# Two token tiles placed by matrix multiplies instead of by indirect DMA in an attention and mixture-of-experts kernel, and three copies moved from ScalarE to VectorE

## The reference

```python
# layer 0: attention, 16 heads of 8 features, no projections
xh = x.reshape(B, T, 16, 8)
c = xh - mean(xh, axis=1)
attn = softmax(c @ c.T per head) @ xh
x = layernorm(x + attn)
# layer 1: experts, E=64, K=8, NG=8, TG=4, CAP=128
scores = sigmoid(x @ gate.T)              # routing: top 4 of 8 groups, then top 8 experts
w = scores[top8] / scores[top8].sum() * 2.5
# each expert takes its first 128 tokens in token order ("pos" < CAP), the others are dropped
h  = silu(xe @ w1.T) * (xe @ w3.T)        # xe: expert x slot x feature, F = 64
ye = h @ w2.T
out = sum over experts of w * ye at the token  +  shared expert (silu, 128 wide)
x = layernorm(x + out)
```

## Time and profile before

| engine | busy us | share of span |
|---|---|---|
| PE | 415.4 | 75% |
| DVE | 378.3 | 69% |
| ACT | 365.9 | 66% |
| POOL | 351.1 | 64% |

### The profile page before, as it was taken

The page is one execution under the profiler, slowest core; times in us unless marked ns, Lnnn a source line. Parts: engine busy times, 40 slices in busy tenths (PEclk is TensorE's granted clock), DMA queues, the critical chain, the costliest instruction groups (busy, mean ns, idle before and its releaser), DMA issues.

```text
span 550.8 us, 9934 instructions
## 1 busy us (share of the span) xinstructions
PE 415.4 (75%) x3461; PEld 185.7 (34%) x3476; DVE 378.3 (69%) x1390; ACT 365.9 (66%) x486; POOL 351.1 (64%) x374
## 2 busy tenths in 40 slices
PE   3799998999898898898899889645699988740000
PEld 2323333333333333333333322123566666530000
DVE  7632769769769768768868638579877887730095
ACT  2699998998998898898998999610223322210056
POOL 3500000677777777777777777777768778888454
PEclk9699999999999999999999999965999999975555
DMA  3499990111000000000100100102366656334796
GB/s 95 139 220 222 349 388 20 52 40 46 24 6 21 14 3 19 12 3 2 27 3 2 26 3 1 24 2 63 78 121 101 112 92 96 36 36 38 150 291 194
DMA packets 71771, 43.69 MB, mean 79 GB/s; under 512 B 11859, under 2 KB 70964, under 8 KB 71329
## 3 DMA queue, kind: packets, MB, share of 16 engines
q1 hardware_dynamic: 51744, 36.18, 24.0%
q0 software_dynamic: 19968, 6.75, 10.5%
HBM read 21.27 MB, written 41.24 MB: 113 GB/s over the span
## 4 chain that ended last, share of the span: by engine, by line
DVE 29%; PE 23%; POOL 16%; ACT 14%; issue 9%; DMA 7%; ACTq 0%; DVEq 0%; POOLq 0%; SPq 0%
POOL records L571 10%; ACT large L1005 9%; PE PV L743 7%; PE S L727 5%; POOL sums L588 5%; DVE large L1587 4%; DMA sums<-centred,target 4%; PE M L645 3%; DVE LR L1261 2%; DVE centred L1644 2%; DMA records<-rec,index 2%; ACT OT L992 1%; PE M L674 1%; DVE last_stats L1672 1%; PE M L668 1%
## 5 line engine op out<-in xcount | busy, mean ns | idle before, releaser
L571 POOL DMA_INDIRECT records<-rec,index x224 | 225.4, 1006 | 141.0 <-DVE index L1404 70.4
L1005 ACT ACTIVATE large<-S,shift 128x1024 f32<-128x1024 f32 x256 | 273.4, 1123 | 23.3 <-PE S L727 21.1
L743 PE MATMUL PV<-large,V 128*9 128x512 f32 x1024 | 135.2, 600 | 0.0
L588 POOL DMA_INDIRECT sums<-centred,target x64 | 99.3, 1552 | 24.9 <-issue 12.2
L727 PE MATMUL S<-LR 64*128 64x512 bf16 x512 | 100.7, 392 | 13.4 <-ACT large L1005 9.0
L727 PEld LDWEIGHTS S<-LR 64*128 64x128 bf16 x512 | 24.6, 93 | 155.1 <-ACT large L1005 98.5
L863 PE MATMUL S<-large 128*128 128x512 bf16 (+1 forms) x189 | 42.6, 375 | 10.0 <-DVE large L1587 6.7
L1261 DVE COPY LR<-M 128x1024 bf16<-128x1024 bf16 x49 | 33.4, 681 | 16.9 <-PE M L645 16.9
L1587 DVE TENSOR_SCALAR large<-slot_c,large 128x128 bf16<-128x128 bf16 x256 | 43.7, 283 | 0.0
L1057 ACT COPY AK<-S 128x512 f32<-128x512 f32 (+1 forms) x17 | 9.5, 560 | 33.6 <-PE S L871 33.6
L863 PEld LDWEIGHTS S<-large 128*128 128x128 bf16 x204 | 19.1, 100 | 29.6 <-issue 9.8
(11 more groups left out here) (207 smaller groups left out, 672.1 us busy)
## 6 DMA issues: line engine op xcount, KB each, us to landing
records<-blank SPq DMA_DIRECT2D x1, 6176.0 KB, 32.2
large<-sums SPq DMA_DIRECT2D x24, 256.0 KB, 5.4
X<-records SPq DMA_DIRECT2D x15, 386.0 KB, 4.4
sums<-blank SPq DMA_DIRECT2D x2, 2112.0 KB
large<-L_ffn_w_dram SPq DMA_DIRECT2D x2, 2048.0 KB, 11.0
records<-rec,index POOLq DMA_INDIRECT x224, 2.1
X<-L_attn_x_dram SPq DMA_DIRECT2D x8, 256.0 KB, 2.9
w2s<-L_ffn_w_dram SPq DMA_DIRECT2D x1, 2048.0 KB, 17.5
```

What stands on the lines that cost most here:

```text
L571: pool.indirect_dma_start(records, bass.IndirectOffsetOnAxis(ap=index[:, i * TOP + k:i * TOP + k + 1], axis=0), rec[:, i, :], None, bounds ...
L588: pool.indirect_dma_start(sums[n % SUMS], bass.IndirectOffsetOnAxis(ap=target[:, u, i:i + 1], axis=0), ye[:, u, i, :], None, bounds_check= ...
L743: mm = pe.matmul(PV[g % 2][32 * i:32 * i + VCOLS, :], V[:, b % 2, 2 * c + k, QUAD * g + i, :], E[:, u % 2, i, k, :], start=c == 0 and k == ...
L1005: nc.scalar.activation(E[:, u % 2, 2 * (i // 2):2 * (i // 2) + 2, i % 2, :], S[:, 2 * (n % 2):2 * (n % 2) + 2, :], ACT.Exp, bias=shift[:, ...
```

## The change

The last two token tiles of batch 6 are no longer scattered. `scatter` issues 16 DMAs for batch 6 instead of 32, and `scatters_for` counts two tiles. Instead, `place_x` and `find_rows` go over 6 tiles (`PLACED`) instead of 4. VectorE prepares the two tiles in the last attention period (`late_tiles`, 12 instructions), and ScalarE builds their 0/1 matrix (`late_hot`): for each tile and expert the absolute difference of slot row and slot (`Abs`, with the slot as a per-partition operand), then one `Relu(1 - x)` over the whole step. The splitting of batch 7's weights in three parts is done before step 0 for 12 experts only and for the other 52 during steps 1 to 3 (`first_rows`, `far_rest`, `far_low` and two ScalarE copies). The store into `Z` now comes behind that splitting, and the matrix of step 1 is built inside step 0. The parts are kept in `Z` and `slot_of` in the memory of `AK`. In every attention period the three copies named above go from ScalarE to VectorE.

```diff
@@ constants
+LATE = 2
+PLACED = LATE + TILES
+HOTS = 4
+FIRST_WV = 3
-NORM_SLOT, X1T_SLOT, EXP_SLOT, SIGMOID_SLOT = 3, 5, 6, 7
-ACT_TAKES = {6: 15}
+NORM_SLOT, EXP_SLOT, SIGMOID_SLOT = 3, 6, 7
-VALUE_SLOT = 12
@@ scatters_for, scatter
-            sent = TILES * min(expert + 1, TOP)
+            sent = (TILES - LATE) * min(expert + 1, TOP)
...
+                tiles = TILES - LATE if p == BATCHES - 2 else TILES
                 for k in range(TOP):
-                    for i in range(TILES):
-                        n = k * TILES + i
+                    for i in range(tiles):
+                        n = k * tiles + i
@@ TensorE: place_x, find_rows
-                wait_next(pe, hot, s + 1)
-                if s == 0:
-                    pe.wait_ge(x_split, 4)
-                for k in range(PARTS):
-                    for i in range(TILES):
+                wait_next(pe, hot_late, s + 1)
+                for i in range(PLACED):
+                    if i >= LATE:
+                        wait_next(pe, hot, s * TILES + i - LATE + 1)
+                    if s == 0 and i == 0:
+                        pe.wait_ge(late, LATE_STEPS)
+                    if s == 0 and i == LATE:
+                        pe.wait_ge(x_split, 4)
+                    for k in range(PARTS):
                         pe.matmul(S[:, u % 2, 0:n * CAP], x_parts[:, k, i, :],
...
+                if s == FIRST_WV + 1:
+                    pe.wait_ge(wv_far, 6)
                 for e in range(experts_of(s)):
-                    for i in range(TILES):
+                    for i in range(PLACED):
@@ ScalarE: attention period
-                    if slot == VALUE_SLOT and b + 1 < BATCHES:
...
-                        build_v(b + 1)
-                    if phase != "last":
-                        for j, at in ACT_TAKES.items():
-                            if slot == at:
-                                take_turned(phase, b, j)
...
-                        if slot == X1T_SLOT:
-                            copy_x1T(phase, b)
@@ ScalarE: the matrix of the two tiles
+            def late_hot(s, u):
+                n = experts_of(s)
+                if s == 0:
+                    act.wait_ge(unit_weighed, UNITS * BATCHES)
+                    act.wait_ge(late, LATE_SLOTS)
+                if s >= HOTS:
+                    wait(act, found_done, s - HOTS + 1)
+                for i in range(LATE):
+                    for e in range(n):
+                        k = STEP_FIRST[s] + e
+                        ins = nc.scalar.activation(one_hot[:, u % HOTS, i, e, :], slot_c[:, :], ACT.Abs,
+                                                   bias=slot_of[:, i, k:k + 1])
+                ins.then_inc(late_far, 1)
+                wait(act, late_far, s + 1)
+                both = one_hot[:, u % HOTS, 0:LATE, 0:n, :]
+                nc.scalar.activation(both, both, ACT.Relu, bias=1.0, scale=-1.0).then_inc(hot_late, 1)
+
             copy_quad(BATCHES - 1, QUADS - 1)
             norm_start(BATCHES - 1)
+            late_hot(0, 0)
             copy_x1T("epilogue", BATCHES)
             exp_logits("epilogue", BATCHES, BATCHES - 1)
             exp_gate("epilogue", BATCHES, BATCHES - 1)
+            late_hot(1, 1)
             gate_sigmoid(BATCHES - 1)
+            late_hot(2, 2)
@@ ScalarE: expert steps
                 if s + 1 < STEPS:
                     copy_x(s + 1, s + 1)
                     exp_step(s + 1, s + 1)
+                if s + 1 == FIRST_WV - 1:
+                    act.wait_ge(wv_far, 2)
+                    nc.scalar.copy(part_of(FAR, TILES_7, 0), wv32[:, :, :, FAR]).then_inc(wv_far, 1)
+                if s + 1 == FIRST_WV:
+                    act.wait_ge(wv_far, 4)
+                    nc.scalar.copy(part_of(FAR, TILES_7, 1), wv_rest[:, :, :, FAR]).then_inc(wv_far, 1)
+                if s + 3 < STEPS:
+                    late_hot(s + 3, s + 3)
@@ VectorE: attention period
+                if with_post:
+                    copy_x1T(phase, b)
+                if with_prep:
                     take_turned(phase, b, 1)
...
+                if phase == "last":
+                    late_tiles(p, t)
                 if with_prep:
                     take_turned(phase, b, 5)
+                    build_v(b + 1)
                     prep_shift(phase, b, q, w.step, w.after)
...
                 if with_prep:
+                    take_turned(phase, b, 6)
                     take_turned(phase, b, 7)
@@ VectorE: before and in the expert steps
             one_hot_step(0, 0)
+            last_record(p, t)
             post_shared_out("epilogue", BATCHES, p)
-            last_record(p, t)
-            one_hot_step(1, 1)
...
-            take_weights(0, 0)
             for s in range(STEPS):
                 add_one(s, s)
+                if s == 0:
+                    one_hot_step(1, 1)
+                    take_weights(0, 0)
+                if s == 1:
+                    first_rows(BATCHES - 1, lambda name, ins: ins.then_inc(wv_far, 1), FAR)
+                if s == FIRST_WV - 1:
+                    far_rest()
+                if s == FIRST_WV:
+                    far_low()
                 silu_step(s, s)
+                if s < EARLY_STEPS:
+                    weigh_step(s, s)
                 if s + 2 < STEPS:
                     one_hot_step(s + 2, s + 2)
-                weigh_step(s, s)
+                if s >= EARLY_STEPS:
+                    weigh_step(s, s)
                 if s + 1 < STEPS:
                     take_weights(s + 1, s + 1)
```

More of the change, by code:

```diff
@@ L308, in post_norm_block @@
         x_split = sem("x_split")
+        late = sem("late")
+        hot_late = sem("hot_late")
+        late_far = sem("late_far")
+        wv_far = sem("wv_far")
         pos_done = sem("pos_done")
@@ L979, in build_v @@
                                tokens_of(X, b).rearrange("p (i h d) -> p i h d", i=TILES, h=HEADS)).then_inc(v_built, 1)
-            def take_turned(phase, b, j):
-                bank, n = job(phase, b, f"lr{j}")
-                wait(act, written[bank], n + 1)
-                nc.scalar.copy(LR[:, j, :, :].rearrange("p a t -> p (a t)"), Mb[bank]).then_inc(read[bank], 1)
             def copy_quad(b, g):
@@ L1279, in post_x1, with copy_x1T @@
                                                       ALU.subtract, ALU.mult))
+            def copy_x1T(phase, b):
+                bank, n = job(phase, b, "xt")
+                wait_next(dve, written[bank], n + 1)
+                v.tensor_copy(x1T[:, :], M[bank][:, :]).then_inc(read[bank], 1)
             def post_shared(phase, b, p, t):
@@ L1546, in last_slot @@
                 dve.wait_ge(pos_read, 1)
-                t.step("slot", v.scalar_tensor_tensor(slot_of[:, :, :], ie(mask), -float(CAP), ie(pos), ALU.mult, ALU.add))
+                t.step("slot", v.scalar_tensor_tensor(slot_of[:, TILES_7, :], ie(mask), -float(CAP), ie(pos),
+                                                      ALU.mult, ALU.add))
             def last_record(p, t):
@@ new lines, in first_rows @@
+            def first_rows(p, step, experts):
+                ie = lambda a: a[:, :].rearrange("p (i e) -> p i e", i=TILES)
+                n = experts.stop - experts.start
+                step("recw", v.tensor_tensor(wv32[:, 0, :, experts], ie(scores)[:, :, experts],
+                                             wsum[:, :].unsqueeze(2).to_broadcast([P, TILES, n]), ALU.mult))
+                token = record_of(p)[0][:, :, TOK_COL].unsqueeze(2).to_broadcast([P, TILES, n])
+                step("row", v.scalar_tensor_tensor(wv32[:, 1, :, experts], ie(pos)[:, :, experts], float(ALL_TOKENS),
+                                                   token, ALU.add, ALU.subtract))
@@ L1581, in one_hot_step @@
                     wait(dve, post, post_at(BATCHES - 1, "slot"))
[L1582 to L1584 removed]
+                if s >= HOTS:
+                    wait(dve, found_done, s - HOTS + 1)
+                for i in range(LATE, PLACED):
                     for e in range(n):
                         own = slot_of[:, i, STEP_FIRST[s] + e:STEP_FIRST[s] + e + 1]
[L1587 to L1588 removed]
+                        ins = v.tensor_scalar(one_hot[:, u % HOTS, i, e, :], slot_c[:, :], own, None, ALU.is_equal)
+                    ins.then_inc(hot, 1)
             split_x(p, t)
```

117 lines of the change are left out of this document (81 added, 36 removed).

## The result

The changed kernel takes 568.42 us (median of four runs, 567.44 to 569.91), the kernel before 552.71 us beside it: 1.029 times as long, 95% interval 1.025 to 1.033. The profiled execution took 568.53 us with a span of 566.7 us. The forecast was 567 us.

What follows compares the result with a forecast made beforehand. The end was taken to hang on POOL's last add, through the adds' start and POOL's 7.4 us a step. Later adds, +16.2 us, with the copies' -1.0 gave +15.2 on 552.3: 567.5, forecast 567 us, range 549 to 575.

Steps and rivals of the forecast that it cites:

- Part 1: POOL, batch 6: sixteen scatters less free POOL at 372.3 instead of 393.4 us; alone worth nothing.
- Part 2: Attention periods: three copies leaving ScalarE gain only in the first period, -1.0 us (bounds -13.3 to +3).
- Part 3: Last attention period: VectorE's twelve preparing instructions, 4.9 us, fall where it waits for PE; value 0, bounds 0 to +2.
- Part 4: Step 0: the store into Z comes 3.0 us later; first add at 396.8 us, +3.1.
- Part 5: Expert steps: ScalarE's matrix joins the dependency ring, which becomes 8.2 us (7.5 to 9.0), above POOL's 7.4.
- L: Expert steps: length of the nine new ScalarE instructions per step, 3.5 us, bounds 2.8 to 4.3.
- Steps 1 to 3: Early expert steps, each with one matrix in its path: silu of step 3 at 418.5 us.
- The sum: Whole kernel: last add starts at 532.2 instead of 516.02 us, +16.2; with Part 2 +15.2.
- A: Rival: ScalarE bounds the attention periods, so all three copies come back in seven periods; 555.2 us, chance 0.12.
- B: Rival: POOL stays the bound of the expert steps, with a matrix of 2.7 us; 549 us, chance 0.15.
- D: Rival: end unchanged, scatters were hidden beside VectorE and matrices fit ScalarE's idle time; 552 us, chance 0.06.
- C: Rival: step ring longer still, by the two-operand price or PE falling to half clock; 578 us, chance 0.07.

Runs made afterwards that it cites:

- all scatters: The changed kernel with all 32 scatters of batch 6 on POOL again, PE's placing kept: 568.94 us.
- second Relu: The changed kernel with a second Relu over the same 1024 columns in each of ScalarE's matrices: 586.76 us.
- matrix behind the copy: The changed kernel with ScalarE building step s+3's matrix behind the copy of X, ahead of the up product's exponential: 558.98 us.
- copies alone: The kernel before with only the three copies of a period moved from ScalarE to VectorE: 553.93 us, ratio 1.001.
- early-split version: Matrix behind the copy, plus step 0 placed early, matrices of steps 1, 3 and 4 moved or cut, far weights split before step 0: 549.10 us.

## Why the prediction was right, step by step

**Part 1, sixteen scatters less.** Right: the last one starts at 371.35 us, and POOL then waits 24 us. Worth nothing in the changed kernel (all scatters: 568.94), worth 5.0 us where nothing else is late (554.14 against 549.10), through the loads and not through POOL.

**Part 2, the copies.** The period stays at 42.5 us, as argued from the releasers. My -1.0 us for the first period isn't confirmed: 553.93 us, interval 0.998 to 1.004. A few of the runs scatter by 3 us, so a gain of half a microsecond remains possible.

**Part 3, the two tiles.** Right. VectorE works on them from 347.78 to 352.3 us, 4.5 us, and the last quad is read after only 0.60 us of idle time for PE:

```profile
353.47 0.26 DVE L1175 RECIPROCAL rden<-PV 128x16 f32<-128x16 f32 x1 [0.60 <-PE PV L770]
```

**Part 4, step 0.** The first add comes at 396.35 us; predicted was 396.8 less part 2, 395.8. The first scatter of this execution came 1.4 us earlier than in the earlier trace rows, so I count from there: PE's start was predicted at 286.7 us and is at 286.4, the first add was predicted at 299.7 and is at 300.7. The start is right, but the placing took 1.0 us longer:

```profile
382.03 6.43 PE L884 MATMUL S<-large,Z 128*128 128x512 bf16 x18 [5.01 <-DVE Z L1415]
```

I had given the half clock 7 matmuls, as the earlier trace rows have it, and 5.4 us in all. But PE now waits 5.01 us before it starts, instead of 2.38, and 11 matmuls run at a pitch of 0.43 us. The up product ends at 295.4 us all the same, as predicted: PE's start is 0.4 us early, and I had put 0.7 us too much behind the placing. The 1.0 us of the first add arises behind the up product: I had left out its exponential (`add_one` starts 0.5 us after the product's end), and the first add starts 1.13 us after the weighing does (395.22 us) where it is 0.61 us in a full step; why it is longer there the trace doesn't say.

**Part 5, the ring.** Right in place and size: predicted 8.2 us (7.5 to 9.0), measured 8.00 in ten of the eleven rings and 8.89 in the first; L predicted 3.5, measured 3.43; an `Abs` predicted 0.39, measured 0.389; PE's own step predicted 7.25, measured 7.24 where nothing holds it. The second Relu shows that ScalarE's time goes into the ring one to one (9.09 us where the clock stays full), the matrix behind the copy that it is the place and not the amount.

By the Trainium skill, page "ScalarE: Activation LUTs", section "What ACT_TABLE_LOAD costs", an ACTIVATE with one pointer operand takes about 280 + 0.833 N ns, which by estimate is 387 ns for 128 columns; the trace agrees with its 389 ns.

**Steps 1 to 3** came out 2.8 us late. The silu of step 3 was predicted at 418.5 us and runs from 418.99 to 419.87 us. It is the end that has to be compared, since the 3.1 us counted from the last silu to the weighing hold only the compares and that weighing; from the first scatter it is 324.2 us instead of 321.4. Inside there are two terms that I had mis-sized or left out. Timeline of ScalarE and PE:

```profile
396.11 0.28 ACT L1093 ACTIVATE X<-S 128x128 f32<-128x128 f32 x1 [1.47 <-PE S L920]
...
401.05 0.80 PE L933 MATMUL M<-w2s,AK 64*128 64x128 f32 x4 [2.68 <-DVE AK L1727]
...
403.55 1.12 PE L920 MATMUL S<-AK,large 128*64 128x128 f32 x8 [0.25 <-ACT AK L1085]
...
404.88 1.57 ACT L1112 CAST Z<-Z 128x416 bf16<-128x416 f32 x1
406.08 2.49 ACT L1062 ACTIVATE large<-slot_c,AK 128x128 bf16<-128x128 bf16 x8
```

Each copy of the far weights takes 1.57 us where I had put 0.5, and delays the `Abs` behind it by 1.20 us: 1.4 us more in all. And behind PE's wait of 2.68 us its clock is at half: down product, turning, finding and up product of 128-column pieces take 0.80, 1.22, 0.51 and 1.12 us, where the run with the matrix behind the copy has 0.49, 0.71, 0.45 and 0.66 us: 1.3 us that no term of mine held. The up product of step 1, ahead of both, ended at 300.4 us from the first scatter, as predicted.

The same happens once more in the first of the eleven full rings, from the silu of step 3 to that of step 4:

```profile
419.93 0.71 PE L933 MATMUL M<-w2s,AK 64*128 64x128 f32 x8 [1.95 <-DVE AK L1727]
...
421.28 1.98 PE L920 MATMUL S<-AK,large 128*64 128x128 f32 x16
```

The granted clock from 421 to 426 us is 0.66, the up product takes 1.98 us instead of 1.09, and the ring takes 8.89 us.

**The sum.** For the start of the last add +16.2 us were predicted, or +15.2 with part 2, and +16.3 were measured; counted from the first scatter it is +17.8. That the forecast of 567 us came within 1.4 us of the 568.42 is in part luck. Counted from the first scatter, the end of steps 1 to 3 is 2.8 us late, and the eleven rings give 1.3 us of it back: they take 88.9 us instead of 90.2, although one of them is 0.9 us longer than the rest. The mechanism, a ring through ScalarE that outlasts POOL's 7.4 us, is the one that the runs show. The end after it is as before: from the last add to the end of the span 34.4 us against 34.8.

**The rivals.** A is out (copies alone). B did not happen: its condition was an L of 2.7 us, measured 3.43. But it is near what the same instructions give in another order: its 549 us and the 549.10 us of the early-split version meet by chance, since that one also places earlier. D is out by 16 us. Of C, the two-operand price is out (389 ns), and of the half clock the steps show it in step 2 and in the first full ring, not in the ten behind.

## What to carry to other kernels

Before you give an idle engine more work, look at what stands behind the place where you put it: here 3.4 us of ScalarE lay whole in each ring when they stood ahead of an instruction that others waited for, and cost the full steps nothing one instruction earlier, where ScalarE waits for PE for half of them and PE's own work covers the rest. Check the short steps at the beginning apart from the full ones, since a gap that holds the work in one doesn't in the other. And a saving that shows no gain is not refuted by that: the sixteen scatters were worth nothing until the order was mended, and 5 us then. A wait of TensorE has to be priced with the clock behind it, and not by its length alone.

## What the runs showed of the hardware that was not expected

- A ScalarE copy of 416 f32 columns to bf16, written with a stride into the interleaved parts, takes 1.57 us; a copy of the same form on VectorE takes 0.87 us. Both stand in the early-split version:

```profile
381.79 1.59 ACT L1083 CAST Z<-Z 128x416 bf16<-128x416 f32 x1 [4.44 <-DVE Z L1681]
...
384.33 0.87 DVE L1721 CAST Z<-Z 128x416 bf16<-128x416 f32 x1
```

- Whether the clock falls was not a matter of one wait's length. 0.69 us of waiting in each step of the changed kernel left it at full (1.00 from 426 to 512 us). With the second Relu it stayed full behind waits of 1.78 us in three steps and fell behind waits of 1.78, 1.77, 1.78 and 1.14 us in four others (up product 1.82 to 1.98 us instead of 1.09). What tells these apart wasn't tried.
- The times of the attention stretch vary from one execution to the next: in the kernels with the moved copies the first scatter comes at 94.20 to 97.61 us.
